# When VectorE folds in four of the eight experts: pairs of gated sums moved in a software-pipelined step

## The reference, cut to what matters

```python
# 1: cross attention with a top-k, a state-space convolution, and an FFN
scores = einsum('bthd,bghd->bhtg', Q, K) / sqrt(DH)        # 4 heads, 257 context vectors
topv, topi = top_k(scores, 32); probs = softmax(topv)      # the 32 largest of 257
attn_mean = zeros.at[..., topi].set(probs).mean(axis=1)
c_t = attn_mean @ V
y = s4d(layernorm(x) * (1 + g * scale_in) + g * shift_in)  # a convolution, by Fourier transform
xt = x_text + (y * (1 + g * scale_out) + g * shift_out)
x = x + layernorm(xt + gelu(layernorm(xt) @ W1 + b1) @ W2 + b2)
# 2: self attention over 32 tokens (softmax over 32 scores)
x = x + attn(layernorm(x))
# 3: mixture of 8 experts, 2 of them with a gate that isn't zero
gates = top_2_softmax(cosine_scores + x @ w_route.T)
h = gelu(einsum('bsd,edh->bseh', x, w1) + b1)
x = x + einsum('bse,bsed->bsd', gates, einsum('bseh,ehd->bsed', h, w2) + b2)
```

## Time and profile before

| | |
|---|---|
| time, median of 3 runs | 676.73 us (674.57 to 677.14) |
| the profiled execution | 678.07 us, span 676.3 us |
| instructions in the span | 12285 |
| TensorE busy (matmuls) | 586.8 us, 87% |
| VectorE busy | 514.9 us, 76% |
| ScalarE busy | 314.2 us, 46% |
| GpSimd busy | 272.9 us, 40% |
| mean granted TensorE clock | 0.929 of full speed |

### The profile page before, as it was taken

One profiled execution on the slowest core, in us unless ns is written; L12 is line 12 of the kernel. 1 busy time (PEld: TensorE's weight loads), 2 busy tenths in 40 slices (PEclk: granted clock), 3 DMA queues, 4 the chain that ended last, 5 costly groups with the idle time before them and its releaser, 6 DMA issues.

```text
span 676.3 us, 12285 instructions
## 1 busy us (share of the span) xinstructions
PE 586.8 (87%) x4142; PEld 427.9 (63%) x4142; DVE 514.9 (76%) x1769; ACT 314.2 (46%) x793; POOL 272.9 (40%) x630
## 2 busy tenths in 40 slices
PE   0349379898999999999999999999999999988867
PEld 0134233646777777777777777777777767665745
DVE  5479964666797979797979797979797979795533
ACT  5433011414646454545454646464646464635422
POOL 2651310325353535353535353535353535162421
PEclk9968565858999999999999999999999999999988
DMA  5295133030303030303030202030303030000000
GB/s 168 59 282 136 58 125 101 0 100 1 100 9 101 9 101 9 100 10 100 9 101 9 100 10 100 9 101 9 101 9 100 9 100 10 1 9 1 9 1 16
DMA packets 18438, 40.33 MB, mean 60 GB/s; under 512 B 5093, under 2 KB 11190, under 8 KB 17864
## 3 DMA queue, kind: packets, MB, share of 16 engines
q1 hardware_dynamic: 18376, 39.55, 18.6%
HBM read 37.37 MB, written 2.16 MB: 58 GB/s over the span
## 4 chain that ended last, share of the span: by engine, by line
PE 61%; DVE 28%; issue 4%; DMA 2%; ACT 2%; POOL 1%; SPq 1%; POOLq 0%; DVEq 0%
PE D L1058 8%; PE BB L1058 8%; PE BB L1081 8%; PE S L1034 4%; PE D L1075 4%; PE S L1050 4%; PE S L1051 4%; DVE top L828 3%; DVE work L834 3%; PE BB L1135 2%; PE BB L1136 2%; PE PC L1213 2%; PE PC L1120 2%; DVE work L814 2%; PE BB L1152 2%
## 5 line engine op out<-in xcount | busy, mean ns | idle before, releaser
L485 POOL TENSOR_SCALAR var_in<-mv 128x1 f32<-128x1 f32 x64 | 14.0, 219 | 274.0 <-DVE mv L795 146.6
L1075 PE MATMUL D<-expw,ang 128*128 128x256 f32 x256 | 67.9, 388 | 15.3 <-DVE ang L858 14.1
L834 DVE MATCH_REPLACE8 work<-top,work 128x257 f32<-128x257 f32 x192 | 77.3, 411 | 0.0
L1058 PE MATMUL D<-ang,e_w 128*128 128x128 f32 x512 | 71.9, 287 | 0.0
L828 DVE MAX8 top<-work 128x8 f32<-128x257 f32 x192 | 71.4, 413 | 0.0
L1058 PEld LDWEIGHTS D<-ang,e_w 128*128 128x128 f32 x512 | 63.9, 198 | 10.1 <-issue 10.1
L1058 PEld LDWEIGHTS BB<-ang,w 128*128 128x128 f32 x512 | 59.5, 192 | 7.8 <-ACT ang L554 4.6
L1075 PEld LDWEIGHTS D<-expw,ang 128*128 128x128 f32 x256 | 45.9, 190 | 25.4 <-DVE ang L858 17.3
L1058 PE MATMUL BB<-ang,w 128*128 128x128 f32 x512 | 60.0, 275 | 0.1
L1081 PE MATMUL BB<-expw,ang 128*128 128x256 f32 x256 | 57.9, 379 | 0.0
L1050 PE MATMUL S<-ctx_t,qk 128*128 128x257 f32 x128 | 45.0, 436 | 11.5 <-DMA ctx_l<-in_ctx_l 6.0
(11 more groups left out here) (247 smaller groups left out, 1286.0 us busy)
## 6 DMA issues: line engine op xcount, KB each, us to landing
ctx_n<-in_ctx_n SPq DMA_DIRECT2D x16, 768.0 KB
ctx_t<-in_ctxT SPq DMA_DIRECT2D x16, 514.0 KB
ctx_t<-in_ctxT SPq DMA_DIRECT2D x16, 257.0 KB
x_all<-in_x SPq DMA_DIRECT2D x4, 512.0 KB, 5.5
out<-out_sb SPq DMA_DIRECT2D x16, 128.0 KB, 1.7
ctx_l<-in_ctx_l SPq DMA_DIRECT2D x64, 24.0 KB
w<-in_W SPq DMA_DIRECT2D x1, 1024.0 KB
e_w<-in_e_w SPq DMA_DIRECT2D x1, 1024.0 KB, 4.8
```

The costliest lines, as they stand in the source:

```text
L834: V.match_replace(work[:, 2 * q + k, :], top[:, 2 * q + k, 8 * r8:8 * r8 + 8], work[:, 2 * q + k, :], TAKEN).then_inc(chains["taken"], 1)
L1058: ins = MM(bank[:, 128 * m:128 * m + 128], w[:, k, at:at + 128], xs[:, 128 * k:128 * k + 128], start=k == 0, stop=k == 1)
L1075: MM(bank, act2[:, k, :], e_w2[:, k, :], start=True, stop=True).then_inc(s["eo_mm"], 1)
```

## The change

VectorE's order within a step changes for two of the four pairs of gated sums. The pair 0-1 moves from behind the self attention's maximum (L955) to between the first and the second further round of the top-k. The pair 2-3 moves from behind `pT_blk` to behind L955, where the pair 0-1 stood. Pairs 4-5 and 6-7 and the bias stay.

```diff
@@ -933,6 +918,9 @@
                     maxima(a, 1)
                     take(a, 1)
                     top8(a, 0, 1)
+                if dd:
+                    gated(range(0, 2))
+                if a:
                     top8(a, 0, 2)
                 if b:
@@ -944,28 +932,26 @@
...
                 if c:
                     wait(dve, s["s_mm"], one(c))
                     V.reduce_max(nmax_c[:, :], C0[:, D:D + T], AXX, negate=True).then_inc(s["nmaxc_v"], 1)
                 if dd:
-                    gated(range(0, 2))
+                    gated(range(2, 4))
                 if c:
                     wait(dve, s["pc_a"], one(c))
                     V.reciprocal(rsum_c[:, :], sum_c[:, :]).then_inc(chains["rsc"], 1)
...
                     V.tensor_tensor(pT_blk[:, :, :], pT_c[:, :].rearrange("p (o t) -> p o t", o=1).broadcast_to([128, BT, T]), block_mask[:, :, :], ALU.mult).then_inc(s["pt_v"], 1)
-                if dd:
-                    gated(range(2, 4))
                 if a:
                     find8(a, 0, 3)
                     take8(a, 0, 3)
```

```diff
-def wait_apart(eng, sem, value, passed):
...
-    wait(eng, sem, value)
-    if value is not None and not isinstance(value, int):
-        eng.sem_inc(passed, 1)
...
-                wait_apart(dve, chains[f"bn{k}"], tile.count(1, 1), passed_v)
+                wait(dve, chains[f"bn{k}"], tile.count(1, 1))
```

More of the change, by code:

```diff
@@ L53, with __init__ @@
 class Tile:
[L56 to L59, removed]
+    def __init__(self, n):
+        self.n, self.p = n, n % 2
     def count(self, per, more):
[L63 to L66, removed]
+        v = per * self.n + more
+        return v if v > 0 else None
     def half(self, per, more):
[L70 to L73, removed]
+        v = per * (self.n // 2) + more
+        return v if v > 0 else None
 def wait(eng, sem, value):
@@ L293, in build, with tiles @@
         LD_DT, LD_CENT, LD_S4, LD_FILM, LD_W, LD_W2 = 16 * 6, 16 * 11, 16 * 8, 16 * 8, 16 * 17, 16 * 3
-        def tiles(base, first):
-            return [Tile(base, first - k) if not isinstance(base, int) or 0 <= first - k < NT else None for k in range(4)]
+        def tiles(first):
+            return [Tile(first - k) if 0 <= first - k < NT else None for k in range(4)]
         def next_tile(a):
-            return None if not a or (a.static and a.n == NT - 1) else Tile(a.base, a.c + 1)
+            return Tile(a.n + 1) if a and a.n < NT - 1 else None
         def run(step):
             for n in range(1, NT + 3):
-                step(*tiles(0, n))
+                step(*tiles(n))
         block = ctx.enter_context(nc.Block())
@@ L380, in _ @@
                 load(dst, src, to)
[L381 removed]
+            step(Tile(1), None, None, None)
             sp.wait_ge(s["qkw_mm"], 1)
@@ L475, in link @@
                     k[0] += 1
-                    wait_apart(pool, chains[name], tile.count(n, k[0]), passed_g)
+                    wait(pool, chains[name], tile.count(n, k[0]))
                 return link
             def norm(k, tile):
-                wait_apart(pool, s[f"st{k}_v"], tile.count(1, 1), passed_g)
+                wait(pool, s[f"st{k}_v"], tile.count(1, 1))
                 w, h, y, t = (var_in[k][:, i:i + 1] for i in range(4))
@@ L493, in length @@
                 v = mv[3][:, 1:2]
-                wait_apart(pool, s["rs3_g"], tile.count(1, 1), passed_g)
+                wait(pool, s["rs3_g"], tile.count(1, 1))
                 link = links("len", tile, 5)
@@ L664, in sines @@
                 A(ang[:, NP:NPOW, :], ang[:, NP:NPOW, :], ACT.Sin, bias=phase[:, 3:4]).then_inc(s["setup_sin"], 1)
[L666 to L669, removed]
+            transposed(Tile(0))
+            query(Tile(0))
+            keyed(Tile(0))
+            step(*tiles(0), sines)
             act.wait_ge(s["kt_mm"], 1)
@@ L999, in _ @@
             V.tensor_scalar(cent[:, :], cent[:, :], cent_r[:, :], None, ALU.mult).then_inc(s["cent_n"], 1)
-            step(*tiles(0, 0))
+            step(*tiles(0))
             film_bias()
@@ L1239, in film_products @@
                 ins.then_inc(s["film_mm"], 1)
[L1241 to L1245, removed]
+            transposed(Tile(0))
+            query(Tile(0))
+            keyed(Tile(0), 0)
+            keyed(Tile(0), 1)
+            step(*tiles(0), film_products)
             pe.wait_ge(s["ld_w"], LD_W)
```

43 lines of the change are left out of this document (21 added, 22 removed).

## The result

The changed kernel takes 680.5 us (median of 16 runs, 675.96 to 687.68), the kernel before 673.86 us on the same chip (16 runs, 668.69 to 678.53). The ratio is 1.0109, 95% interval [1.0076, 1.0142]: 7.3 us slower, which is also how far the means lie apart; the two medians differ by 6.6 us. Ratios and these means leave out slow executions, which are over 1.5% above the fastest of their kernel: the one of 687.68 us here, and three of 11 of the kernel before (678.02 to 678.92 us) that stood beside the two filled kernels, the query ahead, and GpSimd's addition later. The prediction's ratio was 684.3 / 676.73 = 1.0112. Its time of 684.3 us and the lower end of its range, 681.5 us, lie above what was measured.

The account below looks back on a forecast made before the run. The prediction took each step to be a loop of TensorE's arm and VectorE's arm from L930 to `pT_blk` (L966). 12 x 0.65 = 7.8, + 0.2 - 0.4 = 7.6 us, on 676.73 gave 684.3 us, range 681.5 to 688.5.

Parts of the forecast that it names:

- what bounds a step: VectorE's row from L930 to L966: whatever stands ahead of L966 delays `pT_blk`, which L1204 needs, one for one.
- both pairs: Pair 0-1 behind the top-k's first round: margin 2.4 us, cost 0; pair 2-3 ahead of L966: +0.65 us a step at L1204.
- the exponent: ScalarE's, between L955 and L960: still covered by pair 2-3 with 0.28 us to spare, cost 0.
- the norm: GpSimd's chain behind L951: starts 0.78 us later, L976 doesn't move, cover 1.7 us, cost 0.
- the ends: Behind the twelve full steps: step 15 +0.2 us, steps 16 and 17 together -0.4 us, step 18 0.
- the 0.4 us: Gain in steps 16 and 17, 0.19 us each: experts 6 and 7 no longer wait for pair 2-3.
- the pause: TensorE's wait ahead of L1204 for `pT_blk`: grows from 0.88 us to 1.5 us a step.
- rival 3: TensorE's clock falls from L1204 through L1213 in each step: 2.1 us a step, 26 us more, 710 us; chance 3%.
- the step from the sum to the time: Adding the summed 7.6 us to the median of 676.73 us before, giving 684.3 us, 1.1% slower.
- The 7.6 us: Whole kernel's summed slowdown: 7.8 us in steps 3 to 14, +0.2 in step 15, -0.4 in steps 16 and 17.

Follow-up runs that it names:

- the two filled kernels: TensorE repeats experts 4 and 5's products: once more in the changed kernel (1.0106), twice more with round 3's maxima also ahead of `pT_blk` (1.0298).
- the query ahead: Against the kernel with round 2 of the top-k behind `pT_blk`: next tile's query product ahead of the `pT_blk` matmuls; 659.53 us, 0.9812 to the kernel before.
- GpSimd's addition later: Against the kernel with only pair 2-3 moved: GpSimd adds xt + b2 behind the other tile's norm; 1.0157 to the kernel before.
- the two maxima of round 3: Against the changed kernel: the find half of the top-k's third round also ahead of `pT_blk`; 1.0406 to the kernel before, clean step 34.99 us.
- round 2 behind it: Against the changed kernel: top-k's second round and sum 3 behind `pT_blk`, next FFN's norm and pair 4-5 ahead of round 3; 0.9911 to the kernel before.
- The four orders of VectorE: The change (1.0109), only pair 0-1 moved (1.0084), round 3's maxima ahead of `pT_blk` as well (1.0406), round 2 behind `pT_blk` (0.9911), to the kernel before.
- the fifth: Against the kernel before, only pair 2-3 moved, behind the self attention's maximum: 1.0264, step 34.66 us where 34.34 was expected.

## Why the prediction was right on the step and wrong on the time

**Right: what bounds a step.** "So whatever stands ahead of L966 in its order pushes L966 one for one": `pT_blk` 0.78 us later for one pair, the step 0.65 us longer for the two maxima of round 3, and the reverse with round 2 behind it. The four orders of VectorE that I computed in advance came within 0.03 us a step (34.34, 34.09 for 34.12, 34.99 for 35.0, 33.18 for 33.15); the fifth needed GpSimd's addition out of the way.

**Right: both pairs, the exponent, the norm.** Pair 0-1 has a margin and costs nothing more in its new place, pair 2-3 costs 0.65 us a step at L1204 (now L1190), L960 (now L948) is covered (286.18, no wait), L976 (now L962) doesn't wait for GpSimd, and L979 (now L965) waits 0.57 us (0.6 was said).

**Right: the ends.** From step 15's spectrum product to step 16's it is 0.21 us more (+0.2 was said). In step 16 L1204 stands where it stood and experts 6 and 7 follow at 0.59 us, without their wait for pair 2-3 (TensorE's timeline after; before it was 0.78 us):

```profile
629.24 0.65 PE L1190 MATMUL PC<-ang,pT_blk 128*32 128x64 f32 x32 [1.55 <-DVE pT_blk L954]
629.83 1.13 PE L1061 MATMUL D<-expw,ang 128*128 128x256 f32 x4
```

From step 3 on the profiled changed kernel is 7.9 us longer: 12 x 0.65 + 1.7 for the fall + 0.2, less 1.8 in the tail. Of that 1.8 the 0.4 us are mine; the rest is the clock, which had fallen in step 17 of the kernel before and didn't in this execution.

**A size that was off: the pause.** "359.09 - 357.56 = 1.5 us a step" is 1.72. Experts 4 and 5 start 7.63 us behind the spectrum product (284.49 - 276.86), 0.16 us sooner than the 356.50 of the prediction, and they take 1.03 us. It changes no term of the sum.

**Half right: rival 3.** Its mechanism exists, though not as priced. I had put the lower level on each step, 26 us in all, at 3%. It comes in single steps, at 1.7 us each: one of 36 full steps in the changed kernel, which is 0.6 us per execution, and one of its three steps 15. The rule of the Trainium skill ("TensorE: Matmul & The Clock Gate", section "A second HAM failure mode: psum-queue depth-cycling") holds in this form: with pauses of 2.37 us a step the clock did go down and up again in seven steps of twelve, and filling the pause ended it.

**Wrong: the step from the sum to the time.** "That execution is 1.34 us above the median of 676.73, so for the median I say 676.73 + 7.6". The 7.6 us are inside the measured 7.3 us with its interval of 5.1 to 9.6 us. But 676.73 was the median of three runs, and 16 runs gave 673.86. These 2.9 us are most of the 3.8 by which 684.3 misses 680.5; with 673.86 the same sum gives 681.5. The other 1.0 us, 7.6 against the 6.6 between the medians, is within the interval. The range took "the spread of the median (674.57 to 677.14 before)"; single executions of that kernel go from 668.69 to 678.53. The profile itself could have warned me: its first 174 us, the setup and the first two steps, ran at a mean clock of 0.75, while the full steps ran at 1.00 and agreed to 0.02 us. The two profiles of the kernel before have 5.9 of their 6.0 us there, and over 23 runs the longer ones are those with the lower clock. That the three runs were such long ones by chance is what this suggests; they themselves have no timeline and no clock on record, so the cause of their 2.9 us isn't shown. Why the clock in that stretch differs between executions stays open.

## What to carry to other kernels

In a pipelined loop, look for every place where the leading engine needs something from the one behind, in order of time, and note the slack of each: removing the first stall is worth no more than the slack of the second, here 0.13 us by the rows, and whatever is moved ahead of the second costs its length less what slack is left (0.65 of a pair's 0.78 us here, 0.40 where it had covered ScalarE's exponent). What can wait goes behind the last of these needs, and the leading engine's own free work goes into the pause that remains. And give a time's range the spread of single executions; a median of three is no anchor, above all if the setup and the first steps run at a changing clock.

## What the runs showed of the hardware that I had not expected

- TensorE's clock can fall behind pauses far shorter than a step. No fall in 24 steps with one pause of 0.88 us and in 12 with one of 1.48 us, one in 36 with 1.72 us, three in 12 with two pauses of 0.88 and 0.90 us around one group, seven in 12 with 2.37 us; each costs 1.5 to 1.7 us. In 12 steps with 2.37 us cut to 0.64 by repeated matmuls, none. Step 15 fell in both kernels where it has a pause of 1.77 us for `wsel`, and in one of three profiles of the changed kernel. So a pause makes a fall likelier, but its length alone doesn't decide.
- A VectorE operation with two inputs in SBUF that begins during a GpSimd addition of 0.72 us ends behind it: 0.60 us in place of 0.29. Moving the addition brought the 0.29 back. The Trainium skill, "SBUF — State Buffer", section "SBUF: two separate sides", has the rule: the two engines share a pair of ports, and an operation that needs it waits until the other engine's is through. The trace agrees in that VectorE's operation ends later; it ends 0.14 us behind the addition, which is less than its own 0.29, so that it was held for all of that time isn't shown.
